# A two-layer graph, attention and experts kernel: three store waits handed to the next phase, and the start of the graph hops put in another order

## The reference

```python
xn = _layernorm(x)
x = x + _L0_gnn_ref(xn, ...) + _L0_mix_ref(xn[None], ...)[0]
x = x + _L0_ffn_ref(_layernorm(x)[None], gate, w1, w2, w3)[0]
xn = _layernorm(x)
x = x + _L1_gnn_ref(xn, edge_weight, bias, edge_index) + _L1_mix_ref(xn[None], ...)[0]
x = x + _L1_ffn_ref(_layernorm(x)[None], w_gate, w_up, w_down)[0]
```

```python
deg = segment_sum(ones, col);  dis = maximum(deg, 1.0) ** (-0.5)
# x1 = emotions_feat @ W1 + b1, gnn_out = x1, then four times:
alpha = tanh(x_i @ gw[:D] + x_j @ gw[D:] + gb)     # x_i = x[col] (target), x_j = x[row] (source)
msg = (dis[row] * dis[col])[:, None] * alpha * x_j
gnn_out = gnn_out + segment_sum(msg, col)
```

## Time and profile before

| | |
|---|---|
| median of 3 runs | 2437.07 us (2435.0 to 2440.97) |
| the profiled execution: its time | 2444.96 us |
| its span | 2442.9 us |
| PE busy | 2232.8 us, 91% of the span |
| DVE busy | 1568.5 us, 64% |
| ACT busy | 994.1 us, 41% |
| POOL busy | 253.2 us, 10% |
| mean granted clock of PE | 0.954 |

### The profile page before, as it was taken

One profiled execution on the slowest core, in us unless ns is written; L12 is line 12 of the kernel. 1 busy time (PEld: TensorE's weight loads), 2 busy tenths in 40 slices (PEclk: granted clock), 3 DMA queues, 4 the chain that ended last, 5 costly groups with the idle time before them and its releaser, 6 DMA issues. The chain is left out here.

```text
span 2442.9 us, 33615 instructions
## 1 busy us (share of the span) xinstructions
PE 2232.8 (91%) x12602; PEld 1966.7 (81%) x12602; DVE 1568.5 (64%) x2601; ACT 994.1 (41%) x1549; POOL 253.2 (10%) x258
## 2 busy tenths in 40 slices
PE   6889999995995999985999999969989999989898
PEld 4778999994884787784888888847789999978697
DVE  7635666657867788876999999966633333345422
ACT  4122223225753454534888888840021222221120
POOL 0067773000001000011000000011000000000000
PEclk9989999997997999976999999989999999999899
DMA  4331222114436755055455554145312111234214
GB/s 172 129 88 41 44 45 73 40 48 130 141 120 265 275 215 216 23 170 218 156 190 203 205 188 171 52 160 175 102 39 76 39 40 50 76 116 145 98 43 143
DMA packets 114795, 300.46 MB, mean 123 GB/s; under 512 B 18818, under 2 KB 45818, under 8 KB 114630
## 3 DMA queue, kind: packets, MB, share of 16 engines
q1 hardware_dynamic: 103750, 276.81, 32.6%
q0 software_dynamic: 10880, 21.48, 3.2%
HBM read 295.50 MB, written 124.20 MB: 172 GB/s over the span
## 5 line engine op out<-in xcount | busy, mean ns | idle before, releaser
L2365 DVE TENSOR_TENSOR ex_wl<-exlast,ex_wh 128x1024 fp32r<-128x1024 f32 x216 | 252.9, 1220 | 10.5 <-ACT ex_wh L2432 9.9
L2432 ACT ACTIVATE ex_wh<-exlast 128x1024 fp32r<-128x1024 f32 x216 | 217.9, 1058 | 19.2 <-PE ex_pu L2388 8.6
L1529 DVE TENSOR_TENSOR m_kvf<-m_bank,m_bkv 128x256 f32<-128x256 f32 (+1 forms) x160 | 68.0, 425 | 229.0 <-PE m_bank L1431 206.4
L1188 POOL DMA_INDIRECT scratch_slots<-pay,idx x160 | 197.5, 1234 | 59.4 <-issue 59.4
L1431 PE MATMUL m_bank<-m_w_lo,xh 128*128 128x256 f32 (+1 forms) x1280 | 179.4, 282 | 6.6 <-DVE xr L1572 5.7
L1431 PE MATMUL m_bank<-m_w_hi,xh 128*128 128x256 f32 (+1 forms) x1280 | 177.4, 281 | 0.3
L1431 PE MATMUL m_bank<-m_w_hi,xl 128*128 128x256 f32 (+1 forms) x1280 | 177.1, 280 | 0.0
L1431 PEld LDWEIGHTS m_bank<-m_w_lo,xh 128*128 128x128 f32 (+1 forms) x1280 | 163.5, 186 | 9.2 <-issue 9.0
L1431 PEld LDWEIGHTS m_bank<-m_w_hi,xl 128*128 128x128 f32 (+1 forms) x1280 | 162.4, 186 | 0.2 <-issue 0.2
L1431 PEld LDWEIGHTS m_bank<-m_w_hi,xh 128*128 128x128 f32 (+1 forms) x1280 | 161.4, 186 | 1.1 <-issue 1.0
L1763 PE MATMUL gl_bank<-gl_gh,gl_al 125*125 125x512 f32 x385 | 152.8, 397 | 8.2 <-DVE gl_al L1979 8.2
(11 more groups left out here) (465 smaller groups left out, 5264.3 us busy)
## 6 DMA issues: line engine op xcount, KB each, us to landing
exlast<-in_experts SPq DMA_DIRECT2D x216, 512.0 KB
exfirst<-in_experts SPq DMA_DIRECT2D x112, 512.0 KB, 5.6
scratch_seats<-raw SPq DMA_DIRECT2D x95, 512.0 KB
raw<-in_qkv SPq DMA_DIRECT2D x48, 512.0 KB, 6.1
xr<-scratch_res SPq DMA_DIRECT2D x27, 512.0 KB
xr<-scratch_seats SPq DMA_DIRECT2D x27, 512.0 KB, 3.7
scratch_served<-ex_y SPq DMA_DIRECT2D x27, 512.0 KB
scratch_res<-xr SPq DMA_DIRECT2D x25, 512.0 KB
```

The lines of the kernel that those rows point to most:

```text
L1188: e.indirect_dma_start(dram["slot_rows"], bass.IndirectOffsetOnAxis(idx[:, k:k + 1].bitcast(U32), 0), pay[:, k, :], None).then_inc(scat.se ...
L1529: e.tensor_tensor(f, bank[KVB + s % 3][0:r, 0:W2], bkv[0:r], ALU.add)
L2365: return e.tensor_tensor(wl[:, n % RING], raw[unit[1]], wh[:, n % RING].bitcast(F32), ALU.subtract)
L2432: e.activation(wh[:, n % RING], raw[unit[1]], ACT.Copy).then_inc(high.sem)
```

## The change

It has three parts.

1. **Embedding.** The residual stores of chunks 8 and 9 and the last x1 stores are no longer waited for in `sort_and_embed`. Their signals are handed on; `attention` takes them and waits for them before it first writes `ats`, which lies over `xr`. So that nothing freed is still read, x1 of chunks 8 and 9 is written into the two halves of `xr[:, 2]`, for which chunk 8 waits for the residual store of chunk 6.
2. **Graph hops.** SP loads x1 chunk 0, the first gate weights, x1 chunks 1 to 4, then the gate bias and the rest of x1. DVE waits for the first five chunks only, computes the `ga` dots, the diagonal form, then the reciprocal of the degrees, and only then the `gs` dots and the bias. It waits for the rest of x1 just before `dis`. POOL zeroes `xn` after the first `diag_ready`.
3. **Experts.** Even tiles' results go into `xr[:, 2]` instead of an own buffer. The last store (tile 26) is handed on to `serve`. SP waits for it there before it loads into `xr[:, 2]`, and POOL before its first gather, which moves behind `identity` and `clear_pad`.

```diff
 def sort_and_embed(...)
+        x1_of = lambda c: x1s[:, c % 2] if c < TC - 2 else xa[:, 2, c % 2 * NH:(c % 2 + 1) * NH]
...
-                e.dma_start(x1[tokens(c)], x1s[0:r, c % 2]).then_inc(x1_out[c % 2].sem, 16)
+                e.dma_start(x1[tokens(c)], x1_of(c)[0:r]).then_inc(x1_out[c % 2].sem, 16)
...
-            for c in range(TC - RING, TC):
+            for c in range(TC - RING, TC - 2):
                 e.wait_ge(*x_out[c % RING][c])
-            for c in range(TC - 2, TC):
-                e.wait_ge(*x1_out[c % 2][c])
...
+                if c == TC - 2:
+                    e.wait_ge(*x_out[2][6])
-                e.tensor_tensor(x1s[0:r, b], py[b][0:r], bias[0:r], ALU.add).then_inc(evicted.sem)
+                e.tensor_tensor(x1_of(c)[0:r], py[b][0:r], bias[0:r], ALU.add).then_inc(evicted.sem)
...
-        p.hand_on(*ahead.loaded)
-    return ahead
+        stored = x_out[0:2] + x1_out
+        p.hand_on(*ahead.loaded, *stored)
+    return ahead, stored
 def graph_layer(...)
-        x1s, x1_last = p.raises("x1", T[:-1], 16), p.raises("x1_last", ["g"], 32)
+        x1_first, x1s = p.raises("x1_first", T[:HALF], 16), p.raises("x1", T[HALF:-1], 16)
+        x1_last = p.raises("x1_last", ["g"], 32)
...
-            e.dma_start(flat(gw[:]), dram["gate_w"][0:1].broadcast_to([P, 2 * NH])).then_inc(gld.sem, 16)
+            for c in T[:HALF]:
+                e.dma_start(g[:, c], dram["x1"][c * TP:c * TP + P]).then_inc(x1_first.sem, 16)
+                if c == 0:
+                    e.dma_start(flat(gw[:]), dram["gate_w"][0:1].broadcast_to([P, 2 * NH])).then_inc(gld.sem, 16)
             e.dma_start(gb[:], dram["gate_b"].broadcast_to([P, HOPS])).then_inc(ld.sem, 16)
-            for c in T[:-1]:
+            for c in T[HALF:-1]:
                 e.dma_start(g[:, c], dram["x1"][c * TP:c * TP + P]).then_inc(x1s.sem, 16)
...
             e.memset(zero, 0.0).then_inc(blank.sem)
+            e.wait_ge(*diag_ready["first"])
             e.memset(xn, 0.0).then_inc(consts.sem)
...
-            e.wait_ge(*x1s[TC - 2])
-            e.wait_ge(*ld["gb"])
+            e.wait_ge(*x1_first[HALF - 1])
...
             e.wait_ge(*gld[0])
-            dots(gs, 1, 0, HALF)
-            e.drain()
-            bias(0, 0).then_inc(bias_ready.sem)
             dots(ga, 0, 0, HALF)
+            e.memset(deg[:], 1.0)
             e.wait_ge(*consts["ident"])
             e.drain()
             halve(0)
             spread(0).then_inc(diag_ready.sem)
-            e.memset(deg[:], 1.0)
-            e.wait_ge(*x1_last["g"])
             e.wait_ge(*degrees["degrees"])
-            e.drain()
             e.tensor_scalar(deg[0:TP], bank[7][0:TP, 0:TC], 1.0, None, ALU.max)
             e.drain()
             e.reciprocal(rdeg[:], deg[:]).then_inc(rdegrees.sem)
+            dots(gs, 1, 0, HALF)
+            e.wait_ge(*ld["gb"])
+            e.drain()
+            bias(0, 0).then_inc(bias_ready.sem)
             e.wait_ge(*root["root"])
...
             e.tensor_scalar(z[:], z[:], -0.5, 1.5, ALU.mult, ALU.add)
+            e.wait_ge(*x1s[TC - 2])
+            e.wait_ge(*x1_last["g"])
             e.drain()
             e.tensor_tensor(dis[:], dis[:], z[:], ALU.mult).then_inc(scales.sem)
 def experts(...)
-        y = p.sb("y", [P, 2, D])
+        y = [xr[:, 2], p.sb("y", [P, D])[:]]
...
-            for b in range(2):
-                e.wait_ge(*y_out[b][NTILE - 1 - (NTILE - 1 - b) % 2])
+            e.wait_ge(*y_out[1].last())
...
-        p.hand_on(*ahead.loaded)
-    return ahead
+        p.hand_on(*ahead.loaded, y_out[0])
+    return ahead, y_out[0]
 def serve(...)
             for u in range(SLOTS + 2, KC):
                 w.load(e, w_dram, u)
+            e.wait_ge(*served_last.last())
             load(2)
...
-            gather(0)
             identity(e, ident, consts)
             clear_pad(e, xh, xl)
+            e.wait_ge(*served_last.last())
+            gather(0)
             for c in C[1:]:
                 gather(c)
```

More of the change, by code:

```diff
@@ L715, in _ @@
                     e.wait_ge(*x1_out[b][c - 2])
-                e.tensor_tensor(x1s[0:r, b], py[b][0:r], bias[0:r], ALU.add).then_inc(evicted.sem)
+                if c == TC - 2:
+                    e.wait_ge(*x_out[2][6])
+                e.tensor_tensor(x1_of(c)[0:r], py[b][0:r], bias[0:r], ALU.add).then_inc(evicted.sem)
                 e.drain()
                 t = slot(c)[0:r, 0:NH]
-                e.tensor_tensor(t, t, x1s[0:r, b], ALU.add).then_inc(summed.sem)
+                e.tensor_tensor(t, t, x1_of(c)[0:r], ALU.add).then_inc(summed.sem)
                 for i in range(2 * c, min(2 * c + 2, NP)):
@@ L729, in _ @@
                     e.memset(pay[:, :, 3], 0.0)
-        p.hand_on(*ahead.loaded)
-    return ahead
+        assert [c % RING for c in (TC - 2, TC - 1)] == [0, 1] and 6 % RING == 2
+        stored = x_out[0:2] + x1_out
+        p.hand_on(*ahead.loaded, *stored)
+    return ahead, stored
 def project(nc, tag, at, xh, xl, w_dram, base, out, raw, first, at_stored, base_stored, then, xr):
@@ L1320, in _, with attention @@
                 e.tensor_copy(counted, cacc[:, 0:NBUCK * TP]).then_inc(counts.sem)
-def attention(nc, tag, xh, xl, at, w_dram, bq_dram, bkv_dram, softly, raw, first, then, ats, ats_free, beside=None):
+def attention(nc, tag, xh, xl, at, w_dram, bq_dram, bkv_dram, softly, raw, first, then, ats, ats_free, beside=None, taken=()):
     PAIRS, W2 = KC, 2 * P
@@ L1329, in attention @@
     with Phase(nc, tag) as p:
-        p.take(*first.loaded)
+        p.take(*first.loaded, *taken)
         w = Weights(p, raw, 3, D)
@@ L2327, in store_y @@
                 e.wait_ge(*served_[i])
-                e.dma_start(served[i * P:(i + 1) * P], y[:, i % 2]).then_inc(y_out[i % 2].sem, 16)
+                e.dma_start(served[i * P:(i + 1) * P], y[i % 2]).then_inc(y_out[i % 2].sem, 16)
             def load(i, u):
@@ L2461, in _ @@
                     e.wait_ge(*spent[i, u])
-                    e.activation(y[:, i % 2], flat(py[:]), ACT.Copy).then_inc(served_.sem)
+                    e.activation(y[i % 2], flat(py[:]), ACT.Copy).then_inc(served_.sem)
                     if i + 1 < NTILE:
@@ L2495, in _, with serve @@
                     split_h(i + 1)
-        p.hand_on(*ahead.loaded)
-    return ahead
-def serve(nc, tag, xh, xl, served, answer, share, w_dram, bias_dram, bias2_dram, res, raw, first, res_stored, then, xr):
+        p.hand_on(*ahead.loaded, y_out[0])
+    return ahead, y_out[0]
+def serve(nc, tag, xh, xl, served, answer, share, w_dram, bias_dram, bias2_dram, res, raw, first, res_stored, then, xr, served_last):
     with Phase(nc, tag) as p:
@@ L2517, in serve @@
         SLOTS = 4
-        p.take(*first.loaded, *res_stored)
+        p.take(*first.loaded, *res_stored, served_last)
         w = Resident(p, KC, D, first.raw, SLOTS, first)
@@ L2845, in build @@
             with normed(0) as (xh, xl):
-                ahead = sort_and_embed(nc, xh, xl, io["x"], io["w1"], io["b1"], x1, res, graph, idx, pay, spill, raw,
+                ahead, x_stored = sort_and_embed(nc, xh, xl, io["x"], io["w1"], io["b1"], x1, res, graph, idx, pay, spill, raw,
                                        io["qkv0"], xr)
                 ahead, at_stored = attention(nc, "m0", xh, xl, at, io["qkv0"], io["bq0"], io["bkv0"], True, raw, ahead,
-                                             io["wo0"], ats, (), lambda e, p: scatter(e, p, graph, idx, pay, 0, EK))
+                                             io["wo0"], ats, x_stored, lambda e, p: scatter(e, p, graph, idx, pay, 0, EK), x_stored)
         with sb("counts", [P, TC, N], U16) as cnt:
@@ L2870, in build @@
                     res_stored = early_stored + res_stored
-                    ahead = experts(nc, "ex", seats, served, io["experts"], plan, exraw, units_in, xr, res_stored, raw,
+                    ahead, served_last = experts(nc, "ex", seats, served, io["experts"], plan, exraw, units_in, xr, res_stored, raw,
                                     graph["weights"])
@@ L2874, in build @@
             ahead, res_stored = serve(nc, "se", xh, xl, served, answer, share, graph["weights"], io["gnn_bias"],
-                                      io["bo1"], res, raw, ahead, res_stored, io["qkv1"], xr)
+                                      io["bo1"], res, raw, ahead, res_stored, io["qkv1"], xr, served_last)
             ahead, at_stored = attention(nc, "m1", xh, xl, at, io["qkv1"], io["bq1"], io["bkv1"], False, raw, ahead,
```

## The result

| | before | change |
|---|---|---|
| median of ten runs | 2437.28 us | 2430.39 us (2423.92 to 2433.77) |
| ratio | | 0.9971, 95% interval 0.9960 to 0.9983 |
| the same again, on another occasion (six runs, e8 below) | 2438.2 us | 2430.14 us, ratio 0.9966, interval 0.9954 to 0.9978 |

The change makes the kernel 6.9 us faster in the first measurement and 8.3 in the second. I had forecast 11.5 us: the range (2420.0 to 2432.5) holds the time, the sum does not hold the gain. Of the bounds of the parts alone (7.5 to 13.0 us) the first gain lies outside and the second inside; what brings the first into the range is its widening for the spread of runs and the clock. 0.29% lies at the very bound of 0.3% that I had set for "can be told from no change".

The account below looks back on a forecast made before the run. PE was taken to set the pace in hops and attention, so gains lie at three seams between phases. 3.9 + 6.0 + 2.2 - 0.6 = 11.5 us off 2437.07 gave 2425.6 us, range 2420.0 to 2432.5.

Parts of the forecast that it names:

- First seam, 3.9 us: Embedding to attention: no longer waiting for the last stores gains 3.9 us, all of which reaches the kernel's end.
- my lower value: Embedding to attention: gain of 3.25 us, from SP's 3.5 us wait less two more semaphore clears.
- the bracket: Embedding to attention: last store to next DMA, 5.51 us, less 1.33 of a seam without store wait; gain 4.2 us.
- Hops, 6.0 us: Start of the graph hops: first tanh 6.0 us earlier, 3.9 from DVE's idle time and 2.1 from overlap.
- the first rival: Hops' start: late x1 costs 1.6 us, DVE's bias blocked by POOL's zeroing 0.6; hops gain 3.8, total 2427.8; chance 0.15.
- the quiet stretch: Hops' loads: two microseconds at 55 GB/s before x1 streams, blamed on the gate bias; if x1's own, 1.6 us less gain.
- I cost it at nothing: Hops' start: POOL's 4.36 us zeroing of xn, moved beside the source dots, was taken to cost nothing.
- Third seam, 2.2 us: Experts to serve: handing on the last store gains 2.2 us, between 1.8 by SP's wait and 2.6 by the bracket.
- Clears, 0.6 us: Outside the two store seams: five more semaphore clears at 0.12 us each lose 0.6 us.
- besides those in the two seams, two more stand behind the projection: Barrier behind the projection: two additional semaphore clears at 0.12 us each, as part of the 0.6 us lost.
- The waits that come back: Attention's first split and serve's first mix wait for loads instead; no gain at store seams, total 2431.7; chance 0.11.
- PE's clock: Attention rounds: the earlier start makes PE's clock fall, 1.8 us lost in each of 15 rounds, total 2452.6; chance 0.03.

Follow-up runs that it names:

- e8: The change again, unedited, beside the kernel before on another occasion; 2430.14 us, ratio 0.9966 to the kernel before.
- e1: Only the change's embedding part (with its call) put into the kernel before; ratio 0.9995 to the kernel before.
- e10: Only the embedding part in the kernel before, with the skipped overflow stage's unroll factor UN cut from 8 to 4 (short stage); ratio 0.9986 to before.
- e5: The change without the new wait ahead of POOL's zeroing of xn, so the zeroing runs early again; ratio 0.9962 to the kernel before.
- e2: Only the change's graph layer part put into the kernel before; ratio 0.9969 to the kernel before.
- e9: The change with the skipped overflow stage's unroll factor UN cut from 8 to 4 (short stage); ratio 0.9948 to the kernel before.
- e4: The change with one empty drain more at the end of DVE's block in the embedding; ratio 0.9959 to the kernel before.

## Why the prediction was right or wrong

**First seam, 3.9 us: 3.4.** SP's wait less two clears, my lower value, was the better measure. I had left 1.33 us for what remains, the bracket of a seam with three clears; 2.08 remain here, 0.75 us more. The trace of the change shows where: SP still runs two satisfied waits and a branch between its last store (until 136.86) and its drain at the barrier (137.51), 0.65 us where the seam that I compared with has 0.06, and POOL's three clears with their drains take 0.90 us where they took 0.68. "The 3.9 us reach the end" was wrong for the kernel as it is: by the profiles some 2 us of them are lost again before the graph layer in e1, and with the short stage of e10 only the two clears.

**Hops, 6.0 us: 6.0 to 6.6 at the first tanh** (24.60 and 24.24 to 18.04 and 18.20). The order of the steps came out as worked out. The five chunks of x1 were there 8.3 us after the phase's first DMA (737.65); I had said 8.7 (746.5), the first rival 10.7 (748.5), so its half on x1 falls. DVE still waited 0.86 us, more than the 0.5 that I had named and less than the 1 us that was to speak for the rival, since its sums were done earlier than assumed. That the gate bias caused the quiet stretch was not tried by itself. DVE's bias was held by the zeroing, 0.77 us in the row and 0.70 by e5: "I cost it at nothing" was wrong, and the first rival right in this half. What I had held against it does not bear: the count sum at 745.33 starts after the old zeroing has ended (739.68 + 4.36 = 744.04); the earlier sums did run beside it, but none is a `tensor_scalar`. That the count sum starts on time instead of 1.6 us late made up for the bias; I had taken its late start as given, and that the sum came out is luck to that extent: e2, where the late start stays, gains 5.5 to 5.9 us. Over the six profiles of kernels with the new start and the zeroing where the change has it, the phase takes 319.9 us on average, over six with the old one 326.3: 6.4 us less, so the gain does reach the phase's end.

**Third seam, 2.2 us: 1.8**, SP's wait less its clears again, of which some 0.4 may go in `serve`. The mix had no idle time, as said; what came later than forecast were the weight slices, which I had not followed past the first mix.

**Clears, 0.6 us: about 1.2.** Behind the projection they take 0.3 us (e9), at the seam ahead of the MLP 0.3, at the other seams together 0.1. At the very end, from SP's last DMA to the end of the span, it is 5.29 and 5.34 us in the two profiles of the change and 4.81 in both of before, 0.5 us more. The three clears that I put at the end of the program stand, by POOL's rows, two ahead of the MLP and one at the end.

**The step that failed** is "besides those in the two seams, two more stand behind the projection": for that place I counted clears and took the rest of the barrier as it was. It is 2.1 us longer. 0.3 of that are the two clears; the rest comes because DVE's program is two instructions longer, so that its jump over the skipped stage lands two instructions later and the standstill falls on the signal that the barrier waits for. From the last store of the projection to the first tanh it is 24.3 us in the change, 22.8 with the standstill at its old place and no clears more (e2), and 22.0 without it (e9). With the parts as measured, 3.4 + 6.4 + 1.8 - 0.4 (`serve`) - 0.9 (clears other than behind the projection) less 2.1 is 8.2 us, against 6.9 and 8.3 measured.

**The other rivals.** The waits that come back: at the attention's start none did; in `serve` 0.4 us at the most that the averages show. PE's clock: the first attention takes 420 us with and without the change, and both profiles of the change have one fall of the clock of 3.4 us inside its rounds, as the first profile of before has.

## What to carry to other kernels

Where the program jumps over code, count what lies behind the jump: a few instructions more or less far ahead of it can move a standstill of two microseconds onto a barrier, and shortening the skipped body by one constant takes it away. When a part of a change gains less than its own stretch shows, measure every stretch between phases in both profiles, also those it doesn't touch. A single pair of profiles differed by 13 us in a stage that was the same in both; a second profile of before is the cheapest run of a study.

## What the runs showed of the hardware

Code arrives by DMA while the kernel runs. The page of the change lists two queues for it (packets, MB, share of the 16 engines), as the page of before does:

```profile
q8 instruction: 100, 1.64, 0.3%
q14 instruction: 65, 0.53, 0.1%
```

In the change's standstill, 726.5 to 729.0 us, the only traffic of the whole core is on the second of them:

```profile
DMA packets 2, 0.02 MB, mean 7 GB/s; under 512 B 0, under 2 KB 0, under 8 KB 0
...
q14 instruction: 2, 0.02, 2.1%
```

65 packets of together 0.53 MB are 8.2 KB each. The Trainium skill, page "Trainium Architecture — The Big Picture", section "The software stack", gives 64 bytes for an instruction, which would make 128 of them a packet. The same section has the runtime bring the streams into the engines' memory when the program is loaded; these rows show packets during the execution, so here not all of a program is there from the start.

This fits all the landings, if such a packet is one block of DVE's program: on 1505 and 1507, in the block that ends at 1507, the next block is missing three and one instructions later (standstill 2.2 and 2.6 us); on 1508 the landed block is missing itself (2.9 us for the jump); on 1403, in the block that ends at 1507 as well, 105 instructions are left and nothing is waited for.

The traces also speak for a block of 128 that is asked for ahead. I count on from the instruction behind the standstill in steps of 128 recorded DVE instructions, which gives 18 places up to the end. In the change at 7 of them a packet of this queue begins 0.66 to 0.74 us after DVE has started the instruction there, so it brings something that lies further on; with the count begun one instruction later it is 5 places, and with any other start at most 2. In e8 it is 9 of 18 at the same start, and in e9 the start that stands out is the one 105 instructions behind the landing (6 of 18; the others at most 2). No run varied the block's size or the length of the jump by itself.

What stays open is the end of the standstill. In the change the last packet has landed at 727.55, and DVE goes on at 729.0; before it is 737.9 and 739.3, in e4 726.5 and 728.0. So 1.4 to 1.6 us of each standstill pass with no packet for the core on any queue that brings code to these engines, and the rows don't say which of the packets is DVE's.
